# A transformer block on one core: score units in longer runs within a step

## What is computed

```python
xn = _layernorm(x, axis=-1)                      # x: 16 sequences x 256 tokens x 128
q = _lora(xn, Wq, Aq, Bq)...; k = ...; v = ...   # 16 heads of 8
s = jnp.einsum('bhqd,bhkd->bhqk', q, k) / math.sqrt(DH)
s = s + alibi[None] + mask                       # causal
p = jax.nn.softmax(s, axis=-1)
o = jnp.einsum('bhqk,bhkd->bhqd', p, v)
s = o @ Wp.T
# 8 experts of hidden size 512, each token sent to the one with the largest logit
g = _silu(_L0_ffn_ref(xn, W1, b1, W2, b2, Wr, br))
x = x + s * g
```

## Time and profile before

| what | value |
|---|---|
| median of 3 runs | 296.31 us (295.81 to 296.85) |
| the profiled execution's own time | 296.07 us |
| its span, first to last instruction | 294.2 us |
| PE busy | 267.8 us, 91% |
| DVE busy | 228.1 us, 78% |
| ACT busy | 185.5 us, 63% |
| POOL busy | 152.6 us, 52% |
| mean granted TensorE clock | 0.983 |

### The profile page before, as it was taken

How to read it: one execution, slowest core, us unless ns; L and a number is a source line. 1 busy time by engine, 2 the same in 40 slices (tenths; PEclk the granted TensorE clock), 3 DMA queues, 4 the chain that set the end, 5 groups by cost and what they waited for, 6 DMA issues and landing times.

```text
span 294.2 us, 12787 instructions
## 1 busy us (share of the span) xinstructions
PE 267.8 (91%) x5196; PEld 203.6 (69%) x5196; DVE 228.1 (78%) x483; ACT 185.5 (63%) x331; POOL 152.6 (52%) x226
## 2 busy tenths in 40 slices
PE   7899999684996999999999999999999999979962
PEld 3556555353674788888887888888788888856641
DVE  3788999789987578596868768685875868676996
ACT  3335355444466668777777778777776876558960
POOL 3073293115436577866677667667766533343100
PEclk9999999979999799999999999999999999999997
DMA  4799556687415442332425433231524623108553
GB/s 137 207 240 212 127 166 194 203 240 225 112 36 134 109 126 67 95 97 57 108 55 129 123 101 84 74 91 51 133 51 96 147 54 90 30 29 250 138 163 111
DMA packets 50970, 35.98 MB, mean 122 GB/s; under 512 B 5112, under 2 KB 48376, under 8 KB 50784
## 3 DMA queue, kind: packets, MB, share of 16 engines
q1 hardware_dynamic: 46680, 28.89, 37.0%
q0 software_dynamic: 2496, 5.12, 7.0%
q10 hardware_dynamic: 1736, 1.15, 1.6%
HBM read 15.28 MB, written 6.75 MB: 75 GB/s over the span
## 4 chain that ended last, share of the span: by engine, by line
PE 68%; DVE 18%; issue 6%; DMA 3%; POOL 2%; SPq 1%; ACT 1%; ACTq 0%; DVEq 0%; POOLq 0%
PE bank L1359 14%; PE bank L1367 12%; PE bank L1273 11%; PE bank L1324 10%; PE bank L1183 4%; DVE row_max L812 4%; PE bank L1281 3%; PE bank L1343 3%; PE bank L1253 2%; PE bank L1190 2%; DVE xn_all L1063 2%; PE bank L1351 2%; DVE w_slots L977 2%; DVE xn_all L1057 1%; DVE o_turned L1020 1%
## 5 line engine op out<-in xcount | busy, mean ns | idle before, releaser
L812 DVE TENSOR_REDUCE row_max<-bank 128x2 f32<-128x512 f32 (+3 forms) x176 | 105.6, 627 | 19.2 <-PE bank L1261 16.3
L757 ACT ACTIVATE probs<-bank 128x512 f32<-128x512 f32 (+1 forms) x176 | 89.5, 558 | 46.4 <-PE bank L1281 46.1
L1273 PE MATMUL bank<-qk_stack 64*64 64x64 bf16 (+3 forms) x1024 | 60.8, 237 | 6.5 <-ACT probs L757 3.3
L1253 PE MATMUL bank<-qk_stack 64*64 64x64 bf16 (+3 forms) x1024 | 61.7, 237 | 1.1 <-DMA qk_stack<-parts 0.7
L554 POOL DMA_INDIRECT expert_rows<-y_slot,token_of x39 | 38.6, 990 | 37.2 <-PE bank L1359 22.8
L532 POOL DMA_INDIRECT xs_slot<-normalised_rows,from_row x39 | 39.7, 1018 | 24.9 <-PE bank L1281 17.9
L1273 PEld LDWEIGHTS bank<-qk_stack 64*64 64x64 bf16 x1024 | 34.3, 108 | 23.6 <-issue 10.7
L739 ACT ACTIVATE w_slots<-w_all 128x1156 f32 x39 | 45.5, 1167 | 4.0 <-issue 3.4
L1324 PE MATMUL bank<-probs,v_diag 128*32 128x64 f32 (+3 forms) x1024 | 46.5, 311 | 1.2 <-issue 1.0
L1045 DVE TENSOR_TENSOR hT<-bank,w_slots 128x512 f32<-128x512 f32 x39 | 27.0, 691 | 23.3 <-PE bank L1359 23.3
L1359 PE MATMUL bank<-xsT_slot,w_slots 128*128 128x128 f32 x312 | 44.6, 286 | 0.2 <-issue 0.2
(11 more groups left out here) (132 smaller groups left out, 346.1 us busy)
## 6 DMA issues: line engine op xcount, KB each, us to landing
qk_stack<-parts SPq DMA_DIRECT2D x120, 64.0 KB, 2.1
qk_stack<-parts SPq DMA_DIRECT2D x32, 128.0 KB, 2.8
w_all<-w_experts SPq DMA_DIRECT2D x8, 512.0 KB, 4.6
x_all<-x SPq DMA_DIRECT2D x7, 512.0 KB, 5.2
normalised_rows<-xn_all SPq DMA_DIRECT2D x4, 512.0 KB, 5.2
xn_all<-expert_rows SPq DMA_DIRECT2D x8, 256.0 KB, 5.2
out<-xn_all SPq DMA_DIRECT2D x7, 256.0 KB, 3.2
xs_slot<-normalised_rows,from_row POOLq DMA_INDIRECT x39, 3.2
```

What stands on the lines that cost most here:

```text
L757: act.activation(probs[:, m % PROBS, 0:w], bank[:, 0:w], ACT.Exp).then_inc(emptied, 1)
L812: dve.tensor_reduce(row_max[b % 2][:, n, pairs[0]:pairs[-1] + 1], bank[:, 0:ln_u * len(pairs)].rearrange("p (c k) -> p c k", k=ln_u), AX.X ...
L1253: pe.matmul(bank[to, c * ln_u:(c + 1) * ln_u], q[rows, p, n * BLK:(n + 1) * BLK], k[rows, p, 0:(n + 1) * BLK], start=(c == 0), stop=False, ...
L1273: pe.matmul(bank[rows, c * ln_u:(c + 1) * ln_u], k[rows, p, kb * BLK:(kb + 1) * BLK], q[rows, p, kb * BLK:], start=(c == 0), stop=False, s ...
```

## The change

From step 3 on, the units of a step are no longer spread over all six turns. Units 0 to 3 stand at the head of turn 0, units 4 to 7 at the head of turn 2, units 8 to 10 at the head of turn 4; turns 1, 3 and 5 have none. All other work stays in its turn. The same units are computed; no instruction of an engine is added or removed. POOL's waits for a unit's scores in a turn without units are put on the last unit of the turn before.

```diff
 GROUPS = ((0, 1), (2, 3), (4, 5), (6, 7), (8, 9), (10,))
 NG = len(GROUPS)
+LONG_GROUPS, LONG_FROM = ((0, 1, 2, 3), (), (4, 5, 6, 7), (), (8, 9, 10), ()), 3
+GROUPS_OF = [GROUPS if i < LONG_FROM else LONG_GROUPS for i in range(NB)]
...
     for i in range(NB):
-        for g, units in enumerate(GROUPS):
+        for g, units in enumerate(GROUPS_OF[i]):
...
                     for t in FETCH_AT.get((i, g), ()):
-                        wait_act_full(pool, "scores", i, units[0])
+                        wait_act_full(pool, "scores", i, units[0] if units else GROUPS_OF[i][g - 1][-1])
                         fetch_rows(t)
...
                             if g in (0, 3):
-                                wait_act_full(pool, "scores", i, units[1])
+                                wait_act_full(pool, "scores", i, units[1] if units else GROUPS_OF[i][g - 1][-1])
...
-                if k < len(GROUPS[g]):
-                    unit_max(i + 2, GROUPS[g][k])
+                if k < len(GROUPS_OF[i][g]):
+                    unit_max(i + 2, GROUPS_OF[i][g][k])
...
                     if i + 2 < NB and (i, g) not in (SLOTS_AT, TILE_EXPERTS_AT):
-                        unit_max(i + 2, units[0])
+                        for u in units[:1]:
+                            unit_max(i + 2, u)
```

## The result

The change makes the kernel slower: 304.3 us (303.5 to 304.7) against 296.6 us for before in the same set of runs, a ratio of 1.027 with a 95% interval of 1.023 to 1.030. The forecast was 301.8 us, in a range of 297.7 to 305.0: right in direction and inside the stated range, 2.5 us short, and outside the narrower range of 299.8 to 303.8 that the prediction gave its own mechanism. The medians differ by 7.7 us.

What follows compares the result with a forecast made beforehand. PE was taken to bound steps 4 to 11, DVE the end. Edges -7.0, two waits +11.5, step 3 -0.1, step 12 +0.1, end +1.2 gave +5.7 us on 296.07: 301.8 us, range 297.7 to 305.0.

Steps and rivals of the forecast that it cites:

- its own mechanism: The main forecast, edges saved against two added waits per step: 301.8 us, range 299.8 to 303.8, chance 0.62.
- Bound: Steps 4 to 11: PE works without idling, so changes to its list and new waits of PE count in full.
- First wait: Turn 0: unit 3 has only three score banks, so it waits for the exp of unit 0, 0.46 us a step.
- Second wait: Turn 2: unit 7 takes over `qk`'s bank and waits for DVE's `remainder`, 1.03 us; lower bound 0.5, upper 1.3.
- What the change takes from PE: Edges between kinds of matmuls in turns 1, 3, 5: 0.94 us in steps 4-6, 0.84 in 7-11, 7.0 in all.
- turns 1, 3 and 5 shorter by less than 0.6 us together: Steps 4 to 11: a listed sign that the prediction is wrong, the three turns saving under 0.6 us together.
- The end: Steps 13 and 14: the last `output` comes after four units, so DVE's closed stretch begins 1.2 us later.
- Step 3: New waits fall into PE's existing 1.7 us wait for fetched rows; turn 5's edges give 0.1, so -0.1 us.
- Waits not there: Rival for the whole kernel: edges won without the waits, so faster; 294.0 us if unit 3 alone waits; chance 0.12.
- only the exps hold: Rival: `remainder` is early enough, unit 7 waits only 0.5 us for unit 4's exp; +1.9, 298.0 us; chance 0.13.
- The clock: Rival: PE's granted clock falls after waits, some 1.7 us a step, eight 13.6; 315 us; chance 0.05.
- More engines late: Rival: turn 3's weights copy or DVE's maxima hold PE again, 0.3 to 0.5 us a step; 305 us; chance 0.08.

## Why the prediction was right, and where it was short

**Bound.** PE's list bounds steps 4 to 11, and each wait added there counts in full: right as far as PE's list goes, which has no idle time there but the waits named below. (In the table the edges are what is left of 6.75 us, so the sum proves nothing by itself; priced turn by turn below they come to 4.3.)

**First wait, unit 3 for the exp of unit 0, 0.46 us a step.** Right: 0.45 (1.70 us for the run, where 0.67 and 0.58 make 1.25), and the run of turn 0 alone shows it by itself.

**Second wait, unit 7 for the bank of `qk`, 1.03 us.** Right: 1.0 us in steps 5 to 11 (the run takes 2.00 us against 1.01), 0.6 in step 4, where the transposes cover part. The run of turn 2 alone costs 0.86 us a step. What lies under it was estimated as the exp alone; moving the projection away showed DVE's maximum of unit 4 there too.

**What the change takes from PE, 7.0 us.** This is the term that was mis-sized: 4.45 us, 0.55 a step and not 0.84 to 0.94. It lies below the prediction's own lower bound of 0.6, and "turns 1, 3 and 5 shorter by less than 0.6 us together" was one of its signs of being wrong: it holds in steps 4 to 10. Turn 1 gave 0.29 against 0.33. In turn 3 of steps 4 to 6 the second tile stood waiting for its weights, the copy that I had put at 10.3 against a start at 10.4: the output ahead of it takes 1.06 us to the next start instead of 0.89, and the `hidden` behind it 0.99, so that 0.05 was left of 0.33.

```profile
131.42 1.06 PE L1370 MATMUL bank<-w_slots,hT 128*128 128x128 f32 x8
132.48 1.16 PE L1362 MATMUL bank<-xsT_slot,w_slots 128*128 128x128 f32 x8
```

ACT's copy ran from 131.26 to 132.43, up to that start. In steps 7 to 11 the v projection has another tile size and kept both edges, so the saving was 0.13, not 0.23. Joining unit 10 gave 0.21 against 0.28, and only 0.09 in steps 7 to 10, where the joined run took 1.43 us instead of the 1.31 of steps 4 to 6 and 11: its last matmuls came late with no wait in the trace. The other two sets show the same place losing a microsecond. That the first chip's 0.12 is a small case of the same thing is likely by its place, not shown.

**The end, +1.2 us.** Right to a tenth up to DVE's last stretch (1.29). Another 0.5 came behind it; the last output projection took 1.24 us in the chain that ended last, where that chain of the kernel before has 0.74 for it. PE had stood for 4.4 us ahead of it and its granted clock was 0.50, the lower level (1.2 GHz), from 298.3 to 299.5; in the kernel before PE had stood for 2.3 us, and the mean clock over its projection (290.3 to 291.1) was 0.89. I had put nothing there.

**Step 3, -0.1 us.** Here the number is luck. The new wait for the remainder took 1.4 us there, and the `hidden` of the first expert tile started 0.9 us later than before (96.58 against 95.71), 0.3 of which was there before the first changed instruction. But the kernel before ran at a clock of 0.59 from 96 to 98 and the changed one at 1.00: before, that `hidden` took 1.38 us to the next start, units 8 and 9 took 1.42 and the value products behind them 1.38, where later steps have 0.99, 0.79 and 0.79. That is 1.6 us, more than the change lost, so the change begins step 4 earlier by 0.45. The clock's part was not in the prediction. Without it the change would have begun step 4 some 1.2 us late, an estimate from these rows.

**The rivals.** "Waits not there" and "only the exps hold" are excluded by the wait for the remainder in steps 5 to 11. "The clock": waits of 0.45 and 1.0 us in a step left the granted clock at 1.00 from step 4 to step 12. What the Trainium skill tells of other kernels there (TensorE: Matmul & The Clock Gate, A second HAM failure mode), a clock that falls back and forth, did not come about here. "More engines late" came true in a small way, 0.2 us in each of steps 4 to 6.

**Not in the prediction at all** was the third cause, which on the first chip is some 0.12 us in each of steps 7 to 10. On the chip of the third set the change is 7.3% slower than before; on that of the second the change itself was not run, and two kernels close to it are 5.7 and 6.4% slower.

## What to carry to other kernels

Before lengthening a run on the bounding engine, walk the rotation of its banks: the run may be no longer than the banks whose reader keeps pace, and the last unit must not take over a bank whose reader stands behind a long chain on its engine. Then price the saved edges one by one: an edge is saved only if what follows has the same tile size and its data is ready at once. And where a gain is about 1%, measure on more than one chip: on the third set's chip, putting wide matmuls back between short ones (unit 10 in turn 5) was worth 4.6 us, more than the edges it costs.

## What the runs showed of the hardware

On two chips PE stood idle for 0.3 to 0.6 us at a time inside or right behind dense stretches of short matmuls, with nearly unchanged durations and mostly with no wait named in the trace. Where such idle times follow each other, PE's restarts are 0.69 to 0.76 us apart in nearly all cases, in all eight runs there (182.27 and 182.98 above are one pair).

The 76 matmuls and 76 weight loads of units 8 to 10 took 1.43 us in steps 7 to 10 on one chip and 2.45 to 2.6 us on the two others; in steps 11 to 13 the same stretch took 1.31 us on all three (the changed kernel, and on the second chip the one with unit 10 alone moved). So the length of the stretch is not the whole condition; what else differs between these steps was not found. The kernel before took 2% longer on those chips than on the first (302.8 and 301.8 against 296.3 us), and the changed one 6.4% longer on the one where it was run (323.7 against 304.3). Moving unit 10 behind wide matmuls removed most of the gaps of turns 4 and 5 and gave 4.6 us.

Why is open. The expectations call it supply: PE would be short of its own instructions. No run measured the supply, and one thing in the trace speaks against supply alone: unit 9's scores in step 7, whose last mask is listed as started at 181.35, reached ACT at 182.35. A group of matmuls that has started needs no further one to deliver its result: PE's last group of the changed kernel on the first chip starts at 298.29, nothing follows it, and DVE reads it at 299.55. One rival can be excluded from the traces kept. The DMA records have 42 loads of 16 KB on the instruction queue in every one of four traces looked at (both kernels, first and third chip). In steps 7 to 10 of the changed kernel on the third chip the first gap of turn 4 ends at the same matmul each time, but 7.0, 5.3, 5.1 and 2.3 us after the last such load began. So these loads do not place the gaps. Another rival stays untested: every run here, the timed ones too, has a span and a clock on record, so all were taken with the recording of the profile on, and none shows whether the gaps are there without it. Nor does a run show why chips differ.
